# A head's maximum taken per bank: attention block on one core, before and after

## The reference

```python
qkv = einsum('bchw,oc->bohw', x, w_qkv)          # 512 -> 3*512
q, k, v = split(qkv); q = q.reshape(b, 8, 64, n) * 64**-0.5
sim  = einsum('bhdi,bhdj->bhij', q, k)           # 8 heads, 1024 x 1024
attn = softmax(sim); out = einsum('bhij,bhdj->bhid', attn, v)
y = einsum('bchw,oc->bohw', out, w_out) + b_out
y = y * rsqrt(mean_c(y*y) + 64**-0.5) * rms_scale
return y + x
```

## Time and profile before

| | us |
|---|---|
| median of 3 runs (lowest, highest) | 4198.86 (4196.45, 4199.99) |
| the profiled execution | 4197.25 |
| its span, first to last instruction | 4195.5 |
| busy: PE / DVE / ACT / POOL | 4085.2 / 2860.5 / 2272.3 / 2856.0 |
| one batch in the middle of the run | 256.97 |

### The profile page before, as it was taken

One profiled execution on the slowest core, in us unless ns is written; L12 is line 12 of the kernel. 1 busy time (PEld: TensorE's weight loads), 2 busy tenths in 40 slices (PEclk: granted clock), 3 DMA queues, 4 the chain that ended last, 5 costly groups with the idle time before them and its releaser, 6 DMA issues.

```text
span 4195.5 us, 53061 instructions
## 1 busy us (share of the span) xinstructions
PE 4085.2 (97%) x18624; PEld 2399.6 (57%) x18624; DVE 2860.5 (68%) x2684; ACT 2272.3 (54%) x3969; POOL 2856.0 (68%) x2204
## 2 busy tenths in 40 slices
PE   7999999999999999999999999999999999999996
PEld 5555555555555555555555555555555555555553
DVE  5667666677666767666676766767667666677765
ACT  3556555565555555555555555645556555455553
POOL 4667676676666767767676676767667676676666
PEclk8999999999999999999999999999999999999998
DMA  3101111111111111111011010111111111111100
GB/s 142 41 32 60 51 41 61 51 45 47 51 60 41 51 41 63 48 41 71 21 66 55 31 71 31 61 51 38 63 50 41 51 41 61 51 51 41 61 21 31
DMA packets 71270, 212.19 MB, mean 51 GB/s; under 512 B 8152, under 2 KB 8280, under 8 KB 58208
## 3 DMA queue, kind: packets, MB, share of 16 engines
q1 hardware_dynamic: 71008, 208.80, 13.9%
HBM read 168.92 MB, written 39.85 MB: 50 GB/s over the span
## 4 chain that ended last, share of the span: by engine, by line
PE 68%; issue 12%; POOL 8%; DVE 6%; ACT 6%; DMA 0%; POOLq 0%; ACTq 0%; DVEq 0%
PE aux L442 15%; PE pv L587 14%; PE score L572 9%; PE aux L499 8%; PE aux L475 7%; PE score L574 7%; PE aux L553 6%; POOL prob_sum L975 4%; DVE maxima L831 2%; ACT probs L656 2%; POOL prob_sum L971 1%; ACT q_hm L665 1%; ACT q_hl L663 1%; ACT q_hl L681 1%; POOL x_lo L285 1%
## 5 line engine op out<-in xcount | busy, mean ns | idle before, releaser
L975 POOL TENSOR_TENSOR prob_sum<-prob_sum,probs 128x512 f32<-128x512 f32 x1536 | 1977.0, 1311 | 459.6 <-ACT probs L656 457.2
L831 DVE TENSOR_REDUCE maxima<-aux 128x1 fp32r<-128x1024 f32 x1024 | 1205.8, 1219 | 891.5 <-PE aux L553 820.5
L656 ACT ACTIVATE probs<-score 128x512 f32<-128x512 f32 x2048 | 1110.6, 594 | 947.5 <-PE score L574 939.9
L587 PE MATMUL pv<-probs,v_sb 128*64 128x512 f32 x4096 | 991.8, 605 | 0.0
L572 PE MATMUL score<-q_hl,k_hh 128*128 128x512 f32 x2048 | 881.6, 430 | 9.9 <-ACT probs L656 8.2
L574 PE MATMUL score<-q_hm,k_l 72*128 72x512 f32 x2048 | 816.7, 399 | 0.0
L971 POOL TENSOR_TENSOR prob_sum<-probs 128x512 f32<-128x512 f32 x256 | 344.6, 1367 | 661.5 <-ACT probs L656 661.5
L442 PE MATMUL aux<-x_hi,w_ring 128*128 128x512 f32 x2048 | 669.6, 408 | 20.0 <-DVE x_lo L285 11.1
L572 PEld LDWEIGHTS score<-q_hl,k_hh 128*128 128x128 f32 x2048 | 387.4, 189 | 276.9 <-issue 174.9
L587 PEld LDWEIGHTS pv<-probs,v_sb 128*64 128x64 f32 x4096 | 248.1, 136 | 482.7 <-issue 431.6
L442 PEld LDWEIGHTS aux<-x_hi,w_ring 128*128 128x128 f32 x2048 | 358.9, 189 | 178.1 <-issue 69.4
(11 more groups left out here) (74 smaller groups left out, 4422.4 us busy)
## 6 DMA issues: line engine op xcount, KB each, us to landing
w_ring<-w_split SPq DMA_DIRECT2D x93, 1024.0 KB, 4.8
x_stage<-x SPq DMA_DIRECT2D x128, 256.0 KB, 4.6
resid<-x SPq DMA_DIRECT2D x128, 256.0 KB, 5.8
out<-resid SPq DMA_DIRECT2D x128, 256.0 KB, 2.0
w_split<-w_ring SPq DMA_DIRECT2D x3, 1024.0 KB, 11.6
w_split<-y_sb SPq DMA_DIRECT2D x3, 1024.0 KB, 3.8
y_sb<-wqkv SPq DMA_DIRECT2D x4, 512.0 KB, 7.9
probs<-wqkv SPq DMA_DIRECT2D x2, 512.0 KB, 7.2
```

Of the source, the lines that this page charges most:

```text
L587: pe.matmul(pv[half][e * D:(e + 1) * D, :], v_sb[:, pair // 2, j, (pair % 2) * P + e * D:(pair % 2) * P + (e + 1) * D], probs[:, j % 4, e, ...
L656: act.activation(probs[:, j % 4, e, :], score[e][:], ACT.Exp, scale=SOFT).then_inc(prob_ready, 1)
L831: dve.tensor_reduce(maxima[:, n:n + 1], bank(k, 2), AX_X, ALU.max).then_inc(aux_free[k], 1)
L975: pool.tensor_tensor(prob_sum[:, e, :], prob_sum[:, e, :], probs[:, j % 4, e, :], ALU.add).then_inc(prob_added, 1)
```

## The change

Head 0's reduction of tiles 0, 1 and 2 (SPLIT_MAXIMA = 3) is taken in two instructions: the item M reduces bank 0, and a new item N reduces bank 1 into a spare column of `maxima`. Each bank has its own aux_full increment and its own release. A new step `join_maxima` at place t = 10 of each slot takes the larger of the three pairs of columns on VectorE and tells T, which waits for it (maxima_joined). Tile 3 and head 1 stay as they were. On TensorE, M's second matmul claims bank 1 for itself, and the output projection claims bank 0 (and 2) before its first matmul and bank 1 (and 3) before its fourth.

```diff
--- before.py
+++ after.py
@@ -34,6 +34,11 @@
 REPEAT_K_AT = {0: ((0, 10), (0, 12)), 2: ((2, 10), (2, 12)), 4: ((4, 10), (4, 12)), 6: ((6, 10), (7, 3))}
 
 EARLY_MAXIMA = (1, 2, 7)
+SPLIT_MAXIMA = 3
+JOIN_MAXIMA_AT = 10
 
 
 
@@ -58,7 +63,10 @@
     preceding = not (first and slot == 0)
     out = []
     if t % 4 == 1 and following:
-        out += [(f"M{t // 4}0", 0), (f"M{t // 4}1", 2)]
+        out.append((f"M{t // 4}0", 0))
+        if t // 4 < SPLIT_MAXIMA:
+            out.append((f"N{t // 4}0", 1))
+        out.append((f"M{t // 4}1", 2))
     if t in (3, 7):
         if slot in (0, 2, 4):
             out.append((f"K{t // 4}", 0))
@@ -85,8 +93,8 @@
     return out
 
 
-PRO_ITEMS = [(6, "K0", 0), (6, "Q", 1), (6, "K1", 2), (7, "M00", 0), (7, "M01", 2), (5, "V0", 0), (6, "V1", 2),
-             (7, "M10", 0), (7, "M11", 2), (7, "V2", 0), (7, "V3", 2), (7, "M20", 0), (7, "M21", 2),
+PRO_ITEMS = [(6, "K0", 0), (6, "Q", 1), (6, "K1", 2), (7, "M00", 0), (7, "N00", 1), (7, "M01", 2), (5, "V0", 0), (6, "V1", 2),
+             (7, "M10", 0), (7, "N10", 1), (7, "M11", 2), (7, "V2", 0), (7, "V3", 2), (7, "M20", 0), (7, "N20", 1), (7, "M21", 2),
              (7, "Q", 0), (7, "M30", 0), (7, "M31", 2), (7, "T", 2)]
 EPI_ITEMS = [(0, "R0", 2), (0, "O0", 0), (0, "O1", 2), (0, "R1", 1)]
 BANKS = 4
@@ -235,6 +243,7 @@
         const_set = sem("const_set")
         mask_set = sem("mask_set")
         mask_ready = sem("mask_ready")
+        maxima_joined = sem("maxima_joined")
         w_hi_set = sem("w_hi_set")
         w_set = sem("w_set")
         spill_hi_set = sem("spill_hi_set")
@@ -412,10 +421,13 @@
                 if body.plan is not pro or n > 0:
                     pe.wait_ge(aux_free[k], n)
                 if two:
-                    other, n = beside_counts(body.plan, body.b, (slot, name))
-                    if body.plan is not pro and pro.end[other] or body.plan is pro and n > 0:
-                        pe.wait_ge(aux_free[other], n)
+                    claim_beside(body, slot, name)
                 return k
+            def claim_beside(body, slot, name):
+                other, n = beside_counts(body.plan, body.b, (slot, name))
+                if body.plan is not pro and pro.end[other] or body.plan is pro and n > 0:
+                    pe.wait_ge(aux_free[other], n)
 
             def wait_w(body, chunk, next_batch):
 
@@ -481,6 +493,7 @@
                     k = claim(body, slot, name)
                     body.consumed(pe, slot, "M30")
                     body.consumed(pe, slot, "M31")
+                    pe.wait_ge(maxima_joined, SLOTS * body.b + slot + 2)
                     if body.plan is pro:
                         pe.wait_ge(mask_set, 2)
                     pe.matmul(bank(k)[:, 0:P], maxima[:], neg_ident[:],
@@ -488,12 +501,14 @@
                 elif name in ("O0", "O1"):
                     done = body.b * SLOTS + slot
                     pair = (slot - 1) % SLOTS // 2
-                    k = claim(body, slot, name, two=True)
+                    k = claim(body, slot, name)
                     if name == "O0":
                         pe.wait_ge(olo_ready, done)
                         if body.first and slot == 1:
                             pe.wait_ge(wo_set, 1)
                     for i in range(2):
+                        if i == 1:
+                            claim_beside(body, slot, name)
                         m = 2 * int(name[1]) + i
                         for n, (w, o) in enumerate(((wo_hi, o_hi), (wo_lo, o_hi), (wo_hi, o_lo))):
                             last = pe.matmul(bank(k + i), w[:, pair, m * P:(m + 1) * P], o[:],
@@ -532,28 +547,37 @@
                 npair, nhalf = divmod(nslot, 2)
                 if it == 0 and slot in EARLY_MAXIMA or body.plan is pro:
 
-                    ks = [claim(body, slot, f"M{it}{e}", two=True) for e in range(2)]
+                    split = it < SPLIT_MAXIMA
+                    ks = [claim(body, slot, f"M{it}0", two=not split), claim(body, slot, f"M{it}1", two=True)]
+                    if split:
+                        claim(body, slot, f"N{it}0")
                     for h in range(2):
                         for e in range(2):
                             rows = slice(e * D, (e + 1) * D)
                             last = pe.matmul(bank(ks[e] + h), q_hi_at(nhalf, e, e, it),
                                              k_hh[rows, npair % 2, e, h * HALF:(h + 1) * HALF],
                                              start=True, stop=True)
-                            if h == 1:
-                                last.then_inc(aux_full[ks[e]], 1)
+                            if h == 1 or split and e == 0:
+                                last.then_inc(aux_full[ks[e] + (h if split and e == 0 else 0)], 1)
                     return
                 if it == (1 if slot in EARLY_MAXIMA else 0):
                     pe.wait_ge(q_repeated, 2 * (body.b * SLOTS + slot + 2))
                     if nhalf == 0:
                         pe.wait_ge(k_repeated, 4 * (body.b * PAIRS + (slot + 1) // 2 + 1))
                 for e in range(2):
-                    k = claim(body, slot, f"M{it}{e}", two=True)
+                    split = e == 0 and it < SPLIT_MAXIMA
+                    k = claim(body, slot, f"M{it}{e}", two=not split)
                     for h in range(2):
+                        if h == 1 and split:
+                            claim(body, slot, f"N{it}{e}")
                         rows = slice(h * D, (h + 1) * D)
                         last = pe.matmul(bank(k + h), q_hi_at(nhalf, e, h, it),
                                          k_hh[rows, npair % 2, e, h * HALF:(h + 1) * HALF],
                                          start=True, stop=True)
-                    last.then_inc(aux_full[k], 1)
+                        if split:
+                            last.then_inc(aux_full[k + h], 1)
+                    if not split:
+                        last.then_inc(aux_full[k], 1)
 
             def scores(body, slot, j):
                 pair, half = divmod(slot, 2)
@@ -626,9 +650,9 @@
             pe.wait_ge(const_set, 4)
             start = Body(pro, -1, True, True)
             for slot, name, _ in PRO_ITEMS:
-                if name[0] != "M":
+                if name[0] not in "MN":
                     item(start, slot, name)
-                elif name[2] == "0":
+                elif name[0] == "M" and name[2] == "0":
                     maxima_of_tile(start, slot, int(name[1]))
             run_bodies(pe, one)
             end = Body(epi, B, False, True)
@@ -828,7 +852,13 @@
                 elif name[0] == "M":
                     k = body.full(dve, slot, name)
                     n = int(name[2]) * IT + int(name[1])
-                    dve.tensor_reduce(maxima[:, n:n + 1], bank(k, 2), AX_X, ALU.max
+                    banks = 1 if name[2] == "0" and int(name[1]) < SPLIT_MAXIMA else 2
+                    dve.tensor_reduce(maxima[:, n:n + 1], bank(k, banks), AX_X, ALU.max
+                                      ).then_inc(aux_free[k], 1)
+                elif name[0] == "N":
+                    k = body.full(dve, slot, name)
+                    n = int(name[1])
+                    dve.tensor_reduce(maxima[:, 2 * IT + n:2 * IT + n + 1], bank(k), AX_X, ALU.max
                                       ).then_inc(aux_free[k], 1)
                 elif name == "T":
 
@@ -868,6 +898,14 @@
                 cols = slice(part * HALF // 2, (part + 1) * HALF // 2)
                 dve.reciprocal(rms_b[:, cols], rms_a[:, cols]).then_inc(inv_ms_ready, 1)
 
+            def join_maxima(body, slot):
+                for i in range(SPLIT_MAXIMA):
+                    body.consumed(dve, slot, f"M{i}0")
+                    body.consumed(dve, slot, f"N{i}0")
+                dve.tensor_tensor(maxima[:, 0:SPLIT_MAXIMA], maxima[:, 0:SPLIT_MAXIMA].bitcast(F32),
+                                  maxima[:, 2 * IT:2 * IT + SPLIT_MAXIMA].bitcast(F32), ALU.max
+                                  ).then_inc(maxima_joined, 1)
             def invert_sums(body, slot, part):
 
                 dve.wait_ge(sums_copied, SLOTS * body.b + slot)
@@ -908,6 +946,8 @@
                                 invert_sums(body, slot, part)
                         if t == NORMALISE_AT[slot] and preceding:
                             normalise(body, slot)
+                        if t == JOIN_MAXIMA_AT and not (body.last and slot == SLOTS - 1):
+                            join_maxima(body, slot)
                         for half in range(2):
                             if (slot, t) in INVERT_AT[half] and not body.first:
                                 invert(body, half, "R", INVERT_AT[half].index((slot, t)))
@@ -937,6 +977,8 @@
             start = Body(pro, -1, True, True)
             for slot, name, _ in PRO_ITEMS:
                 item(start, slot, name)
+                if name == "M30":
+                    join_maxima(start, slot)
```

## The result

The changed kernel takes 4135.05 us (median of 4 runs, 4134.22 to 4136.31), the kernel before 4198.72 in the same comparison (4196.45 to 4199.99): a ratio of 0.9849, with an interval of 0.9832 to 0.9866. It is faster by 63.7 us, where 55 were forecast (4144). The profiled execution took 4134.53, its span is 4132.7.

A forecast was written before the change was run, and what follows sets the result against it. TensorE, busy 97% of the span, was taken as the bound. Gains of 3.38 us a batch, 47.3 over fourteen middle batches, plus 5 and 2.2 made 54.5, say 55 us: 4144 us, range 4125 to 4165.

The forecast's parts named there:

- A plain hold costs 0.22 us: TensorE item behind a tile's scores: 0.12 us lost waiting for its bank, 0.10 more before its second matmul.
- Rival 2: Only the wait goes, the item still restarts as if cold: 0.12 a hold, 29 us in all, 4170; chance 0.12.
- The 512-column reduction at 0.69: VectorE's reduction of one bank was taken to last 0.69 us, between bounds of 0.61 and 1.22.
- The late claim: The projection claims bank 1 at its fourth matmul, at 2005.91, after that bank's reduction ends at 2005.36: free.
- O1's 0.06 back at bank 2: The projection's second half (O1, seventh matmul) waits for bank 2, giving back 0.06 us per projection.
- Slot 6's 0.10 for VectorE: A charge of 0.1 us a batch in slot 6, where an x_lo split and two additions to y also stand.
- The join at 0.6: VectorE's join of the split maxima at 0.6 us, kept for the range in slots 0 and 6; over 1.3 counted as wrong.
- A wait and an increment more inside a pair: TensorE's extra wait and increment in a tile's first matmul pair: costed at nothing, at most one step of 0.23 us.
- Rival 4: The wait inside a pair breaks it in 21 tiles a batch: 77 us more, 55 less, 4221; chance 0.08.
- Slots 1 and 2 set by other engines: GpSimd sets slot 1, gain 0 (at most 0.86 us); VectorE is late in slot 2, gain 0.10 us.
- Rival 1: Slots 1, 2 and 5 pass their holds on as well: 5.2 us a batch, about 82 us, 4117; chance 0.13.
- the first and last batch: First batch gains 5 us, its holds in slots 1 and 2 counting fully; last 2.2, lacking most slot 6 and 7 items.

The follow-up runs named there:

- run 1: The changed kernel, but the output projection claims both its banks before its first matmul, as before the change: 4167.0 us, ratio 0.9926.
- run 4: The changed kernel, with the join as a reduction over pairs of columns with one SBUF input: 4134.83 us, ratio 0.9847.
- run 5: The kernel before, with GpSimd's residual additions in slot 1 cut to 8 of 512 columns: 4188.22 us, ratio 0.9976.
- run 6: The changed kernel, with GpSimd's residual additions in slot 1 cut to 8 of 512 columns: 4114.43 us (two runs), ratio 0.9798.
- run 7: The kernel before, with the split and the join in the prologue alone and the projection's late claim: 4192.8 us, ratio 0.9984.
- Run 2: The kernel before, with the output projection's late claim alone and no split of the reductions: 4198.9 us, ratio 1.0.
- run 8: The changed kernel with Q claiming first, join by reduction, all four tiles split, T later and the masked-maxima wait before a score's second matmul: 4104.47 us, ratio 0.9774.
- run 3: The changed kernel, but item Q claims its bank before it waits for its weights: 4126.04 us, ratio 0.9826.

## Why the prediction was right

**A plain hold costs 0.22 us: right.** Item and second matmul both came back to a step of 0.23. Slots 0, 3 and 4 gained 0.63, 0.64 and 0.61 with three such holds each. Rival 2 (only the wait goes) would have left the second step at 0.33; it is 0.24.

**The 512-column reduction at 0.69: right**, 690 and 679 ns in the groups.

**The late claim: free, and needed.** Its mechanism was as told (bank 1's reduction ends at 1969.58, the fourth matmul starts at 1970.17). That the split without it would leave the projection worse off than before was not in the text; run 1 shows it.

**O1's 0.06 back at bank 2: wrong in size.** The step that failed is "with its weights due a step earlier". The load at 1970.77 is late by that reckoning, and the matmul still starts on time 0.10 behind it. So three holds count 0.66 less 0.02 to 0.05 in slots 0, 3 and 4, and slot 5 gives 0.20 instead of 0.16. In slots 0, 3, 5 and 7 the eighth matmul comes up to 0.03 late on the average of the middle batches, and only where bank 2 comes later, in slot 2, does O1 lose more.

**Slot 6's 0.10 for VectorE: not there.** It gained 0.64, like its neighbours, where 0.50 was forecast. Both terms together make most of the 0.32 by which a batch was under-estimated, 4.5 us over fourteen.

**The join at 0.6: too low, and it made no difference.** It takes 0.87 on the average and 1.30 in slot 4, where 1.3 was named as the point at which the forecast fails. That condition was wrong: run 4 takes 0.72 off each join and the time stays. What the join was expected to wait for, the rest of one GpSimd operation, was right, by the ends of 127 of 128 joins (run 4). The reason given, that the time behind it is free, holds for all slots.

**A wait and an increment more inside a pair: nothing, right.** Rival 4 would have put 21 x 0.23 = 4.8 on a batch; the pair's two matmuls start 0.01 apart and the stretch to the last score matmul is 1.48 against 1.47. The Trainium skill (TensorE: Matmul & The Clock Gate, section "The cost: per-tile semaphore tail") adds 26.3 ns to the tail of a packed group for each increment; the starts of the matmuls show no such time, and no row here shows the end of the pair itself.

**Slots 1 and 2 set by other engines: right, and shown for slot 1.** Runs 5 and 6 cut GpSimd's work and the change then gave 0.88 there. Rival 1 would have had this in the plain kernel. One step was wrong inside it: of the two holds said to be paid back (0.45 and 0.41) only the first went; the second shrank by 0.08, because VectorE reached the second tile late, and the wait for o_lo grew by 0.51. Slot 2 came out at 0.15 for 0.10 by the path forecast: 0.53 won at bank 0, 0.36 given back at bank 2 (the projection's twelve matmuls span 2.99 instead of 2.63). No run changed slot 2 by itself, but the first batch, in which nothing of an earlier one is finished, is a case without that work: there slots 1 and 2 gained 0.85 and 0.84 (31.82 to 30.97 and 31.68 to 30.84).

**The prologue: missed.** The prediction counted slots alone. The same mechanism at 2.4 us, and the clock that comes back with it at 3.7, are the largest error: 5.7 us in run 7. Against it stand the first and last batch, forecast 5 and 2.2 and measured 4.3 and 1.8; slot 0 of the first was 0.34 longer, since 5.5 us of it ran at half clock instead of 4.4. The prologue's first tile also started 1.2 earlier in the profiled execution after, ahead of anything that the change touches; that is chance, since over the ten traces it starts anywhere from 23.77 to 25.69.

**The tail: open.** From the last batch's slot 6 on the profiled execution took 91.9 instead of 89.5. A window of it in the kernel after:
```profile
4062.00:4069.00 7.00, 6.31 (x16) 2.41 (x16) 1.14 (x2) 1.19 (x2) 0.97 (x1) 0.51 0.00 0
```
The clock is at half there, behind a wait for the last maxima that the kernel before has as well, with full clock behind it. Over the eight variants the tail took 89.3 to 92.0. Run 2, whose batches take what they took before, has the same stretch:
```profile
4126.40:4133.20 6.80, 6.22 (x14) 2.40 (x16) 1.03 (x2) 1.19 (x2) 0.96 (x1) 0.50 0.01 2
```
Its tail took 92.0, while runs 1 and 8, which have the split, took 89.7 and 89.3 without that stretch. So the longer tail goes with the clock and is not shown to be the change's; what decides it stays open.

The sum then: 54.5 forecast; middle batches +4.5, first and last -1.1, prologue +7.3, tail -2.4: 62.8, against 62.7 between the profiled executions and 63.7 between the medians.

## What to carry to other kernels

Where a buffer of several banks is released by one instruction, see first whether the next user could start with one bank: split the reader, and let the user claim each bank where it needs it; either half alone gave nothing or only half (runs 1 and 2). Price a short stall at its wait plus the restart of the engine behind it, here 0.12 + 0.10, and count only the stretches where the engine that waits is the last to arrive, since the two slots that GpSimd and VectorE set gave 0.01 and 0.15. Look through the prologue for the same pattern, where nothing covers the wait and the clock can fall behind it.

## What the runs showed of the hardware

- **The order of two waits.** Q, whose second of two waits is the last to be released, starts 0.15 behind that release; with the order swapped it starts 0.05 behind it, which for this one item a slot was worth 9.0 us (run 3). In run 1 the projection, whose late wait is the second of three, starts 0.10 behind its release.
- **A tiny operation with two SBUF inputs.** The join works on 128 x 3 elements and takes 874 ns on the average, as a reduction of one SBUF input 151 (run 4). In slot 4 it lasted 1.30, beside a run of GpSimd additions that start 1.25 apart. The Trainium skill (GPSIMD Engine Reference, section 1, Specifications) names the shared SBUF interface of the two engines; the trace agrees, and adds that an instruction of three columns waits for all that is left of the GpSimd operation in flight (127 of 128 joins).
- **Weights may come late by a little.** A weight load that ended its wait 0.17 late, 0.10 before its matmul, delayed nothing in slot 4; in slots 0, 3, 5 and 7 the matmul after that one came up to 0.03 late.
- **The clock behind an idle time.** In the prologue the granted clock over 36.8 to 42.0 was 0.67 behind an idle time of 1.28 (and one of 0.78 ahead of the tile), and in the changed kernel it stayed at 1.00 behind one of 0.52 (and one of 0.73).
